# Order and banks of the four turned memory readings in the first attention

## What is computed

```
def step(carry, seg):                      # 16 segments of 64 tokens, 16 heads of 128
    mem, z = carry
    sigma_q = elu(qq) + 1.0
    scores = einsum('bhsk,bhtk->bhst', qq, kk) / scale, causal mask
    att_dot = softmax(scores) @ vv
    att_mem = sigma_q @ mem / (sigma_q @ z)
    sigma_k = elu(kk) + 1.0
    delta = vv - sigma_k @ mem / (sigma_k @ z)
    mem_new = mem + einsum('bhsk,bhsv->bhkv', sigma_k, delta)
    z_new = z + sigma_k.sum(axis=-2)
    att = beta * att_mem + (1.0 - beta) * att_dot
    out = att @ Wo
```

## Time and profile before

| what | before |
|---|---|
| median of 3 runs | 751.22 us (750.45 to 751.37) |
| profiled execution, its own time | 748.37 us |
| its span | 746.6 us |
| instructions | 12362 |
| TensorE busy | 651.1 us, 87% |
| VectorE busy | 413.5 us, 55% |
| ScalarE busy | 339.7 us, 45% |
| GpSimd busy | 313.6 us, 42% |
| granted TensorE clock, mean | 0.952 of full speed |
| first attention | about the first 460 us of the span |

### The profile page before, as it was taken

The page is one execution under the profiler, slowest core; times in us unless marked ns, Lnnn a source line. Parts: engine busy times, 40 slices in busy tenths (PEclk is TensorE's granted clock), DMA queues, the critical chain, the costliest instruction groups (busy, mean ns, idle before and its releaser), DMA issues. The chain is left out here.

```text
span 746.6 us, 12362 instructions
## 1 busy us (share of the span) xinstructions
PE 651.1 (87%) x4144; PEld 541.0 (72%) x4144; DVE 413.5 (55%) x1119; ACT 339.7 (45%) x834; POOL 313.6 (42%) x383
## 2 busy tenths in 40 slices
PE   4889989989989989989989986999999619984897
PEld 3668878979979879879879885876666307874564
DVE  6778495394494493692692737662222268455243
ACT  3566757557566556666665651223333302100220
POOL 4665644344353444435421213336665317210563
PEclk9999999999999999999999998999999859995798
DMA  8010110100100100100100313962332242019440
GB/s 271 14 58 29 34 53 1 64 29 3 62 29 25 40 28 28 35 28 28 36 2 1 98 50 107 406 227 85 93 92 78 76 142 86 1 34 357 130 121 19
DMA packets 31313, 57.89 MB, mean 78 GB/s; under 512 B 4670, under 2 KB 17952, under 8 KB 31264
## 3 DMA queue, kind: packets, MB, share of 16 engines
q1 hardware_dynamic: 24256, 42.03, 16.4%
q0 software_dynamic: 4896, 13.12, 6.1%
q10 hardware_dynamic: 2112, 2.10, 0.8%
HBM read 48.06 MB, written 10.09 MB: 78 GB/s over the span
## 5 line engine op out<-in xcount | busy, mean ns | idle before, releaser
L894 DVE RECIPROCAL denominators<-readings 128x2 f32<-128x2 f32 x128 | 21.2, 166 | 148.8 <-PE readings L567 148.1
L567 PEld LDWEIGHTS readings<-memory_copy,sigma 128*128 128x128 f32 x512 | 75.2, 191 | 14.2 <-ACT memory_copy L766 5.4
L427 POOL TENSOR_TENSOR w_high<-xn,ones 128x256 fp32r<-128x256 f32 x84 | 52.5, 655 | 77.0 <-PE ahead L215 35.7
L567 PE MATMUL readings<-memory_copy,sigma 128*128 128x129 f32 x512 | 79.1, 277 | 4.1 <-ACT memory_copy L766 3.8
L775 ACT ACTIVATE memory_reading<-readings,denominators 64x128 f32<-64x128 f32 x256 | 78.5, 356 | 5.2 <-DVE denominators L894 3.1
L766 ACT ACTIVATE memory_copy<-memory 128x258 f32<-128x258 f32 x128 | 50.2, 393 | 62.3 <-PE memory L577 48.2
L900 DVE SCALAR_TENSOR_TENSOR minus_delta<-readings,denominators,v 64x128 f32<-64x128 f32 x240 | 73.8, 347 | 4.2
L577 PE MATMUL memory<-minus_delta,sigma_k_tokens 128*128 128x129 f32 x480 | 73.3, 275 | 0.0
L751 ACT ACTIVATE x<-ahead 128x512 f32<-128x512 f32 x60 | 35.8, 597 | 76.8 <-DVE sigma L883 30.1
L1343 PE MATMUL up_e<-weights_e,xT_e 128*128 x184 | 69.9, 505 | 0.8 <-ACT xT_e L1467 0.8
L1198 POOL DMA_INDIRECT xs_e<-rows_e,gather_at_e x46 | 44.8, 974 | 59.9 <-DVE scatter_at_e L1599 36.1
(11 more groups left out here) (267 smaller groups left out, 1430.0 us busy)
## 6 DMA issues: line engine op xcount, KB each, us to landing
weights_e<-experts SPq DMA_DIRECT2D x24, 608.0 KB, 11.9
xn<-L_attn_Wq SPq DMA_DIRECT2D x8, 512.0 KB, 3.8
xn<-L_attn_Wk SPq DMA_DIRECT2D x7, 512.0 KB, 3.9
xn<-L_attn_Wv SPq DMA_DIRECT2D x7, 512.0 KB, 3.7
wo<-L_attn_Wo SPq DMA_DIRECT2D x1, 2048.0 KB, 12.9
rows_e<-xn ACTq DMA_DIRECT2D x4, 512.0 KB, 8.0
x<-L_attn_x SPq DMA_DIRECT2D x4, 256.0 KB, 3.7
x<-L_attn_x SPq DMA_DIRECT2D x2, 512.0 KB, 3.6
```

Source lines behind the costliest of these rows:

```text
L427: last = pool.tensor_tensor(w_high[i][:, :, of], w_stage[:, :, of], one, ALU.mult)
L567: last = pe.matmul(KQ[g][:, hh * MC:(hh + 1) * MC], sqk[:, GROUP * g + hh, pair, 2 * par:2 * par + 2, :], mz[g][:, hh, :], start=True, sto ...
```

## The change

The turns stand in slots 1, 2, 3 and 4, for heads 0 to 3, and go to banks `local1`, `local0`, `local1`, `local0`. VectorE's adds follow in slots 2, 3, 4 and 5. The waits are written anew: head 1, now the first in `local0`, waits for the mask of slot 1; heads 2 and 3 wait for the adds of heads 0 and 1; the scores of slot 6 wait for all four adds, and the wait between the two turned probabilities of slot 8 goes. The turns after the last stage use the same banks and waits.

```diff
@@ -329,8 +329,8 @@
         OUT_AT = {12: range(0, 3), 13: range(3, 8), 14: range(8, 10), 15: range(10, 16)}
 
         LAST_OUT_AT = {7: range(0, 2), 9: range(2, 6), 11: range(6, 10), 13: range(10, 13), 15: range(13, 16)}
-        READINGS_AT = {1: 0, 3: 1, 4: 2, 5: 3}
-        READINGS_BANK = (1, 1, 0, 1)
+        READINGS_AT = {1: 0, 2: 1, 3: 2, 4: 3}
+        READINGS_BANK = (1, 0, 1, 0)
 
         def all_turns(engine, turn):
 
@@ -627,7 +627,7 @@
                         scores(n, half, 0)
                     if m == 6:
                         if behind:
-                            pe.wait_ge(att_ready, 4 * n - 1)
+                            pe.wait_ge(att_ready, 4 * n)
                         pe.wait_ge(masked, 2 * n + 1)
                         scores(n, half, 1)
                     if behind and m in READINGS_AT:
@@ -636,17 +636,15 @@
                             pe.wait_ge(bt_copied, 4 * n)
                             for g in range(2):
                                 pe.wait_ge(read_ready[g], STEPS * n)
-                        elif h == 2:
+                        elif h == 1:
                             pe.wait_ge(masked, 2 * n + 1)
                         else:
-                            pe.wait_ge(att_ready, 4 * n - 4 + (h + 1) // 2)
+                            pe.wait_ge(att_ready, 4 * n - 4 + h - 1)
                         turn_reading(1 - half, h)
                     if m == 8:
                         pe.wait_ge(p_ready, 4 * n + 2)
                         pe.wait_ge(masked, 2 * n + 2)
                         turn_probs(n, 0, 0)
-                        if behind:
-                            pe.wait_ge(att_ready, 4 * n)
                         turn_probs(n, 0, 1)
                     if m == 12:
                         pe.wait_ge(p_ready, 4 * n + 4)
@@ -719,8 +717,8 @@
                         pe.wait_ge(bt_copied, 4 * n)
                         for g in range(2):
                             pe.wait_ge(read_ready[g], STEPS * n)
-                    elif h != 2:
-                        pe.wait_ge(att_ready, 4 * n - 4 + (h + 1) // 2)
+                    elif h >= 2:
+                        pe.wait_ge(att_ready, 4 * n - 4 + h - 1)
                     turn_reading(1, h)
                 pe.wait_ge(att_ready, 4 * n)
                 pe.wait_ge(y_copied, n - 1)
```

## The result

| what | before | changed |
|---|---|---|
| median of 8 runs | 751.57 us (750.45 to 754.23) | 747.41 us (744.44 to 749.53) |
| profiled execution | 748.37 us | 749.53 us |
| its span | 746.6 us | 747.7 us |

The ratio is 0.9926, with a 95% interval of 0.9908 to 0.9944, a gain of 4 to 7 us; the medians by themselves differ by 4.16 us. Two later comparisons, each on one chip, gave 0.9948 (0.9932 to 0.9965) and 0.9961 (0.9947 to 0.9976), that is 3.9 and 2.9 us. Yet the one profiled execution of the changed kernel is 1.2 us longer than that of the kernel before, and its span 1.1 us. So the stages have to be read by themselves.

A forecast was written before the change was run, and what follows sets the result against it. The prediction took VectorE's progress through slot 7 as the bound: 6 × 0.56 = 3.4 us, with 0 for stage 7 and the end of attention, gives 745.0 profiled or 747.8 us against the median of 751.22; range 744.6 to 750.9.

The forecast's parts named there:

- 0.80 − 0.24: VectorE's slot 7: the add leaving slot 6 saves 0.80, the one entering slot 3 costs 0.24; 0.56 us earlier.
- the overfilled hole: VectorE's slot 3: the entering add of 0.83 exceeds the 0.59 us idle hole, so slots 4 to 6 run 0.24 late.
- the exchange: VectorE's adds: one leaves slot 6 and one enters slot 3, with nothing added or removed in work.
- Stage 7: Stage n = 7, no sigma or projections: add overfills VectorE's slot-3 hole by 0.37; gain 0, bounds −0.3 and +0.4 us.
- the end of attention: After the last stage: output projection could start 0.75 us earlier, but VectorE waits for a transfer; 0, at most −0.1 us.
- Rival 1: Slot 4 and 5 sigmas meet other GpSimd weight splits: −0.12 a stage (750.5 us, chance 0.12) or −1.0 (745.2, chance 0.20).
- the exclusive lock: VectorE instructions with two SBUF inputs and GpSimd share one port pair; the loser blocks for the other's whole instruction.
- Rival 2: TensorE's waits at turns are the gain: 0.36 + 0.38 a stage, 4.4 us in all, 746.8 us; chance 0.06.
- Rivals 3 and 4: Slot 4's two sigma instructions stretch, +2.9 us, chance 0.05; slot 8's wait ended by probabilities, not mask, +1.4, chance 0.03.

The follow-up runs named there:

- a2: Changed kernel with an extra unused VectorE maximum (0.70 us) in slot 6 of stages 1 to 7; stage 54.06 us, ratio to the kernel before 0.9987.
- a3: Changed kernel with an extra unused VectorE maximum (0.70 us) in slot 11; stage 53.55 us, ratio to the kernel before 0.9943.
- b3: Kernel before with an extra unused VectorE maximum in slot 3 of stages 1 to 7; stage 54.08 us, ratio to the kernel before 0.9984.
- a4: Kernel before with turns in slots 1, 2, 4, 5 and banks local1, local0, local0, local1; stage 53.62 us, ratio to the kernel before 0.9954.
- b2: Kernel before with only the four turns after the last stage in alternating banks, waits adapted; stage 54.13 us, ratio to the kernel before 0.9986.
- b4: Kernel before with turns in slots 0, 2, 2, 3 and adds in slots 1, 2, 3, 4; stage 53.42 us, ratio to the kernel before 0.9927.
- c2: Changed kernel a third time, no edit; median 746.25 us, stage 53.46 us, ratio to the kernel before 0.9961.
- b1: Kernel before run again, no edit; stage 54.12 us, ratio to the kernel before 1.0006.

## Why the prediction was right

**The stage.** The forecast was 0.80 − 0.24 = 0.56 us a stage at VectorE's slot 7, and 3.4 us in all. Measured: 0.63 at slot 7 of n = 4, and 4.03 us in six stages; the medians differ by 4.16 us. The first ratio's interval of 4.2 to 6.9 us lies above 3.4, those of the two repeats (2.6 to 5.1 and 1.8 to 4.0 us) hold it. The mechanism was right and the size somewhat small, for two reasons. One is the overfilled hole: the entering add took 0.80, not 0.83, slot 4 was late by 0.23, and by slot 6 only 0.17 were left. That alone gives the 0.58 to 0.62 of n = 2 to 5. The other is a term that the forecast did not have: slot 4's L870, which took 0.66 us in n = 1 and n = 6 before and 0.41 after, so that each of these two stages gained 0.22 more than n = 4 had of it. The prediction read one stage only, n = 4, and took it for all six. a2, a3 and b3 show the exchange by its parts, a4 that its second half may come from another slot.

That 747.8 was named and 747.41 came is in part luck. The median of the kernel before was 751.22 when the prediction was made and is 751.57 with all eight runs, and the three comparisons give 5.6, 3.9 and 2.9 us for one and the same change. The 4.0 us of the stages are the firmer number. The lower end of the range does not follow from its terms either: 745.2 − 0.3 − 0.1 is 744.8, not 744.6. Nothing hangs on that.

**TensorE.** As forecast, the turn of slot 2 had no wait; slot 3's started 3.06 us behind slot 2's reciprocal in both (254.60 to 257.66, 252.93 to 255.99); slot 4's was 0.12 late against the same reciprocal (258.89 − 252.93 = 5.96, before 260.44 − 254.60 = 5.84); slot 6's scores started 0.17 late against slot 2's reciprocal, with a wait of 1.68 instead of "above 1.3"; slot 8's wait is 0.64 where about 0.6 was named.

**Stage 7 and the end of attention.** 0 and 0: 58.10 us from the last full stage's slot 8 to the last reading in both kernels, and 18.68 from there to L140 against 18.65. In n = 7 slot 4's reciprocal came 0.37 us late against slot 2's (411.46 to 414.76, before 415.11 to 418.04), as forecast, and nothing of it is left at the last reading. b2 shows the second alone. The output projection came 0.84 us earlier where 0.7 was named, and the transfer hid it.

**The rivals.** Rival 1, other meetings with GpSimd, fell as it was written, for the two sigma instructions of L885 and its prices of −0.12 or −1.0 us a stage. In n = 4 GpSimd's split began 0.54 us ahead of slot 4's reciprocal instead of 0.30, and the sigma pairs took 1.47 and 1.70 against 1.47 and 1.72. GpSimd in the changed kernel, which has 3.48 for the four L431 against 3.51:

```profile
258.21 2.89 POOL L427 TENSOR_TENSOR w_high<-xn,ones 128x256 fp32r<-128x256 f32 x4 [4.75 <-PE ahead L215]
261.19 3.48 POOL L431 TENSOR_TENSOR w_low<-xn,w_high 128x256 fp32r<-128x256 f32 x4
```

GpSimd's eight splits took 6.46 us together where they had taken 6.28, since the four L427 took 2.89 instead of 2.69. I had argued that the phase could fall either way. For L885 it fell neither way, but for L870 it fell to the good in n = 1 and n = 6. So rival 1's kind of effect was there, in another instruction, in two stages of six, and worth about 0.4 of the 4.0 us. That the split is what lengthened L870 is argued from the overlap in time and was not tried: in n = 4 of the kernel before the split also began 1.03 us ahead of L870, as in n = 1, and L870 took 0.44. All this fits the exclusive lock that the prediction cites as well as it fits sharing, so this case does not decide on that rule. Rival 2 fell with a2: the waits at the turns were gone and so was the gain. Strict rotation of banks is not what pays either, since a4 puts two turns in a row into `local0` and b4 three into `local1`, and both have nearly the same stage. It is a means: it lets the turns come early enough that the adds can use the hole. Rivals 3 and 4 did not happen; the longest L883 is 1262 ns against 1261, and slot 8 is still released by the mask.

## What to carry to other kernels

Where two engines wait for each other in turns, look at the engine that is waited for. Count its work only from its last idle hole to the place where the other engine takes up its result. Moving work from behind that hole into it gains about what the hole holds. Waits removed before that place only reappear in the wait there. Before moving work earlier, ask what it displaces at the start of the chain, as in b4. A part of a per cent is told by the length of the repeated stage in one trace: its mean varied by at most 0.04 us between profiles of one kernel, while the span varied by several microseconds. But read every repetition and not one of them; here two of six stages held a term that the stage I had read did not show.

## What I had not expected of the hardware

The program behind the attention is the same in all twelve profiles (the ten runs above and the first of each kernel), and takes 284.2 to 290.4 us. The windows of the first 30 us behind the attention show a mean granted TensorE clock of 0.83 to 0.94 (1.00 is full speed) in six of them and 0.72 to 0.77 in the other six. Length, busy PE, PEld, DVE, ACT, POOL, then the clock, DMA share and GB/s, for the kernel before, then the changed kernel, then c2:

```profile
460.90:490.90 30.00, 26.70 (x160) 22.76 (x160) 23.36 (x56) 9.75 (x15) 11.26 (x14) 0.89 0.98 379
```

```profile
457.30:487.30 30.00, 27.14 (x148) 23.73 (x149) 20.80 (x51) 8.48 (x13) 11.04 (x14) 0.77 0.98 374
```

```profile
458.80:488.80 30.00, 26.94 (x175) 22.81 (x176) 23.68 (x56) 9.75 (x15) 11.10 (x14) 0.89 0.98 368
```

In the six windows with the lower clock VectorE gets through 50 or 51 instructions instead of 56, and the trace has 144 to 148 matmul records instead of 159 to 177. The mean length behind the attention is 288.6 us for the six with the lower clock (290.4, 287.0, 287.5, 286.7, 289.7, 290.2) and 285.6 for the others (285.7, 284.2, 287.9, 285.8, 285.0, 284.8). The changed kernel had the lower clock there in two of three profiles, the kernel before in none of two, but b2 and b3, whose stages are those of the kernel before but for b3's extra instruction, both had it; so I can't say that the change has a part in it. The lengths overlap, too: b1 took 287.9 with the higher clock, a4 286.7 with the lower. So the clock goes with the length in the mean and does not settle it in a single profile. Twice the low clock came earlier: the output projection (L616) took 10.19 us at a granted 0.71 in a4 and 9.16 at 0.79 in b1, against 7.46 at 1.00. Why the clock falls in one execution and not in the next was not tried and stays open. The first pair of spans stood the wrong way round because the changed kernel lost 290.4 − 285.7 = 4.7 us behind the attention and gained 3.6 before it (460.91 − 457.27). How much of the 4.7 is the clock's is not shown.
